# A bank ring ordered by end of filling, another order of the first loads, and query splitting moved from GpSimd to VectorE

## What is computed

```python
x = x + attention(layernorm(x), Wqkv, Wo)   # 32 query heads of 16, ONE shared key/value head
x = x + ffn(layernorm(x), W_base, b_base, W_gate, A, B)   # base matmul + top-2 of 8 LoRA experts, rank 16
# attention, for each batch b and head h:
#   scores = q @ k.T / 4 + slope[h] * (pos_k - pos_q), causal mask, softmax, @ v; all heads @ Wo
```

## Time and profile before

| what | us |
|---|---|
| median of three runs | 748.17 |
| the profiled execution | 748.7 |
| its span, first to last instruction | 746.9 |
| busy: PE / DVE / ACT / POOL | 686.0 / 557.4 / 359.2 / 228.9 |
| mean granted TensorE clock | 0.975 of full |

### The profile page before, as it was taken

The page is one execution under the profiler, slowest core; times in us unless marked ns, Lnnn a source line. Parts: engine busy times, 40 slices in busy tenths (PEclk is TensorE's granted clock), DMA queues, the critical chain, the costliest instruction groups (busy, mean ns, idle before and its releaser), DMA issues.

```text
span 746.9 us, 13261 instructions
## 1 busy us (share of the span) xinstructions
PE 686.0 (92%) x4304; PEld 309.7 (41%) x4304; DVE 557.4 (75%) x1801; ACT 359.2 (48%) x511; POOL 228.9 (31%) x382
## 2 busy tenths in 40 slices
PE   4689789999998989898989999999999999999997
PEld 2334434444443434343434334344334345555553
DVE  5679788867785868686879999999995175666665
ACT  2202556565554656464656666676676711111111
POOL 0027513132424351424243142143152132222221
PEclk9869999999999999998989999999999999999999
DMA  8641444443312160711070755910000049900001
GB/s 256 156 81 58 94 60 65 83 63 77 129 38 82 38 118 21 128 68 39 16 123 31 110 76 82 127 48 18 17 33 17 16 117 174 189 29 28 29 29 56
DMA packets 38343, 56.32 MB, mean 75 GB/s; under 512 B 6648, under 2 KB 20088, under 8 KB 38144
## 3 DMA queue, kind: packets, MB, share of 16 engines
q1 hardware_dynamic: 33896, 44.98, 32.0%
q0 software_dynamic: 1792, 6.29, 2.5%
q10 hardware_dynamic: 2592, 4.26, 1.6%
HBM read 35.72 MB, written 19.79 MB: 74 GB/s over the span
## 4 chain that ended last, share of the span: by engine, by line
PE 76%; DVE 11%; ACT 5%; DMA 3%; issue 3%; POOL 1%; SPq 1%; POOLq 0%; DVEq 0%; ACTq 0%
PE psum L728 18%; PE psum L680 16%; PE psum L710 11%; PE psum L756 7%; PE psum L627 7%; PE psum L778 6%; PE psum L707 4%; DVE psum L1091 3%; ACT work L913 3%; DVE negm L1096 3%; PE psum L773 2%; PE psum L788 2%; DMA x_sb<-in_x 1%; DMA q_dram<-arena 1%; PE psum L765 1%
## 5 line engine op out<-in xcount | busy, mean ns | idle before, releaser
L913 ACT ACTIVATE work<-psum 128x1024 f32<-128x1024 f32 (+1 forms) x320 | 289.0, 943 | 157.0 <-PE psum L710 122.2
L1091 DVE CUSTOM_DVE_ANT_0 psum<-psum,future 128x384 f32<-128x384 f32 (+3 forms) x512 | 238.8, 514 | 48.0 <-PE psum L680 44.5
L680 PE MATMUL psum<-k_op,arena 106*128 106x512 bf16 (+3 forms) x768 | 216.0, 335 | 26.0 <-DVE negm L1091 8.1
L1096 DVE TENSOR_REDUCE negm<-psum 128x1 f32<-128x512 f32 x256 | 167.2, 687 | 26.8 <-PE psum L680 23.9
L728 PE MATMUL psum<-work,v_op 128*32 128x512 f32 (+3 forms) x1536 | 168.1, 511 | 13.7 <-POOL work L1280 13.7
L1280 POOL TENSOR_SCALAR_AFFINE_SELECT work<-work 128x512 f32<-128x512 f32 x128 | 80.9, 637 | 285.7 <-ACT work L913 285.7
L710 PE MATMUL psum<-arena,k_op 109*128 109x512 bf16 (+3 forms) x640 | 157.6, 317 | 1.9 <-ACT work L913 1.4
L680 PEld LDWEIGHTS psum<-k_op,arena 106*128 106x128 bf16 x768 | 70.6, 98 | 171.3 <-DVE negm L1091 65.0
L627 PE MATMUL psum<-arena,wqkv_sb 128*128 128x256 f32 (+3 forms) x240 | 87.7, 473 | 1.3 <-ACT arena L835 1.3
L707 PE MATMUL psum<-arena,k_op 116*128 116x128 bf16 x512 | 84.9, 223 | 2.7 <-ACT arena L835 1.5
L710 PEld LDWEIGHTS psum<-arena,k_op 109*128 109x128 bf16 x640 | 59.7, 98 | 43.2 <-ACT work L913 13.8
(11 more groups left out here) (87 smaller groups left out, 466.1 us busy)
## 6 DMA issues: line engine op xcount, KB each, us to landing
arena<-q_dram SPq DMA_DIRECT2D x96, 128.0 KB, 5.6
o_dram<-o_sb SPq DMA_DIRECT2D x32, 256.0 KB
q_dram<-arena POOLq DMA_DIRECT2D x16, 384.0 KB, 3.2
arena<-o_dram SPq DMA_DIRECT2D x32, 128.0 KB, 8.8
arena<-rcp_dram SPq DMA_DIRECT2D x32, 128.0 KB, 9.4
out<-wqkv_sb ACTq DMA_DIRECT2D x16, 256.0 KB, 2.0
x_sb<-in_x SPq DMA_DIRECT2D x3, 1024.0 KB, 8.1
work<-in_x SPq DMA_DIRECT2D x3, 1024.0 KB, 16.9
```

The costliest lines, as they stand in the source:

```text
L680: last = nc.tensor.matmul(bank[:, a * width:(a + 1) * width], q_op[0:ROW_MAX, bass.ds(col, P)], k_op[0:ROW_MAX, b, k0:k0 + width], start=T ...
L913: nc.scalar.activation(probs[:, n % 4, heads * hp:heads * (hp + 1), 0:w], src, ACT.Exp).then_inc(exp_done, 1)
L1091: last = nc.vector.tensor_tensor_reduce(keys, keys, future[:, CH - width:CH], -1.0, 3e38, ALU.add, ALU.min, negm[:, late, 0, j * QT + t:j ...
L1096: nc.vector.tensor_reduce(dst, psum[:, bank, 0:len(js) * width].rearrange("p (a k) -> p a k", a=len(js)), AX_X, ALU.max, negate=True).then ...
```

## The change

Five things are changed.

1. `places` hands out banks by a list: a bank goes back to its end when a slot is placed, and for a side item when its last part is placed. With it the planner's extra limit on slots inside a side item goes, so a slot may now stand ahead of every part.
2. Items move: in step 0 chunk 0's queries come first, and two of chunk 1 stand behind the T items of chunk 2; slots of step 0 are spread to its end. The second item of step 4 goes to step 5 and so on, so steps 5 to 9 hold one query item each (before: step 4 two, steps 5 to 8 one).
3. DVE splits items 8 to 15, in steps 3 to 10 behind slot 8; POOL keeps items 2 to 7.
4. All stores of queries are issued by SP instead of POOL, each behind the wait for the store ahead of it.
5. SP's first loads: chunk 3's x comes behind the loads of items 0 and 1; the loads of items 2 to 5 now stand, each behind its store, ahead of `max_rows(1)`. Later loads of items 10 to 15 and of the heads come up to two steps later. DVE splits item 0 two tiles of normalising earlier.

```diff
 AMONG = {
-    0: [("v", 1, None, None)] + [("q", c, m, None) for m in (1, 2, 3) for c in (0, 1)] + tiles_turned(2),
+    0: [("v", 1, None, None)] + [("q", 0, m, None) for m in (1, 2, 3)] + [("q", 1, 1, None)] + tiles_turned(2) + [
+        ("q", 1, 2, None), ("q", 1, 3, None)],
...
-    4: [("v", 3, None, None)] + halves("q", 2, 1) + halves("q", 3, 1),
-    5: halves("q", 2, 2),
+    4: [("v", 3, None, None)] + halves("q", 2, 1),
+    5: halves("q", 3, 1),
...
-        upto = min(NSL - 1, round(NSL * done / (SLOTS_BY * total)))
-        if piece[0] == "side" and piece[2]:
-
-            if k:
-                upto = max(put, min(upto, put + NSB - 1 - inside))
-            inside += len(slots[put:upto])
-        else:
-            inside = 0
+        upto = min(NSL - 1, round(NSL * done / ((SLOTS_BY if k else 1) * total)))
...
+    banks = list(range(NSB))
     for k, order in enumerate(ORDER):
         for what, a, b in order:
...
+            if what == "slot":
+                bank = banks.pop(0)
+                slot_at[a, b] = (bank, last[bank])
+                last[bank] = ("slot", NSL * a + b)
+                banks.append(bank)
+            elif what == "side" and a >= N_FIRST:
+                if b == 0:
+                    bank = banks.pop(0)
                     use_at[a] = (bank, last[bank])
                     last[bank] = ("side", a)
+                if b == len(use_parts(USES[a])) - 1:
+                    banks.append(use_at[a][0])
...
-SPLIT_AT = {(3, 0): 8, (4, 0): 9, (4, 1): 10, (5, 0): 11, (5, 1): 12, (6, 1): 13, (7, 1): 14, (8, 1): 15}
+SPLIT_SLOT = 8
+ON_VECTOR = (0, 1) + tuple(range(8, NCH * PAIRS))
+SPLIT_AT = {3: 8, 4: 9, 5: 10, 6: 11, 7: 12, 8: 13, 9: 14, 10: 15}
...
+            def store_queries(n):
+
+                c, m = Q_ITEMS[n]
+                sp.wait_ge(*split_done(n))
+                if n:
+
+                    sp.wait_ge(q_stored, 16 * n)
+                sp.dma_start(q_dram[c, :, P * m:P * (m + 1)].rearrange("a r q -> r a q"),
+                             qpart[:, n % 4]).then_inc(q_stored, 16)
...
             load_x(2)
+            for n in range(2):
+                store_queries(n)
+                load_queries(n)
             load_x(3)
-            load_queries(0)
-            load_queries(1)
             load_constants(1)
-            step(0)
+            store_queries(2)
+            max_rows(0)
             load_queries(2)
-            load_queries(3)
-            step(1)
-            load_queries(4)
-            load_queries(5)
+            for n in range(3, 6):
+                store_queries(n)
+                load_queries(n)
+            store_queries(6)
+            store_queries(7)
+            max_rows(1)
             load_constants(2)
             load_constants(3)
-            step(2)
             load_queries(6)
             load_queries(7)
+            step(1)
+            step(2)
...
                     step(k, None, (r,))
                     if k % 2 == 0 and r % 4 == 3 and r // 4 < KEY_PIECES:
                         split_keys(k // 2 + 1, r // 4)
+                    if r == SPLIT_SLOT and k in SPLIT_AT:
+                        split_queries(SPLIT_AT[k])
```

More of the change, by code:

```diff
@@ L135 @@
     3: halves("kv", 3) + halves("q", 3, 0),
-    4: [("v", 3, None, None)] + halves("q", 2, 1) + halves("q", 3, 1),
-    5: halves("q", 2, 2),
-    6: halves("q", 3, 2),
-    7: halves("q", 2, 3),
-    8: halves("q", 3, 3),
+    4: [("v", 3, None, None)] + halves("q", 2, 1),
+    5: halves("q", 3, 1),
+    6: halves("q", 2, 2),
+    7: halves("q", 3, 2),
+    8: halves("q", 2, 3),
+    9: halves("q", 3, 3),
 }
@@ L209, in places @@
     slot_at, use_at, last = {}, {}, [None] * NSB
-    e = 0
     for u in range(N_FIRST):
         use_at[u] = (NSB + u % (8 - NSB), ("side", u - (8 - NSB)) if u >= 8 - NSB else None)
+    banks = list(range(NSB))
     for k, order in enumerate(ORDER):
         for what, a, b in order:
[L215 to L221, removed]
+            if what == "slot":
[6 more added lines that the diff above has]
+                    bank = banks.pop(0)
                     use_at[a] = (bank, last[bank])
                     last[bank] = ("side", a)
+                if b == len(use_parts(USES[a])) - 1:
+                    banks.append(use_at[a][0])
     return slot_at, use_at
 SLOT_AT, USE_AT = places()
-SPLIT_AT = {(3, 0): 8, (4, 0): 9, (4, 1): 10, (5, 0): 11, (5, 1): 12, (6, 1): 13, (7, 1): 14, (8, 1): 15}
+SPLIT_SLOT = 8
+ON_VECTOR = (0, 1) + tuple(range(8, NCH * PAIRS))
+SPLIT_AT = {3: 8, 4: 9, 5: 10, 6: 11, 7: 12, 8: 13, 9: 14, 10: 15}
 def uses_behind(k):
@@ L406, in use_count, with split_done @@
             return USES.index((kind, c, m, part)) + 1
+        def split_done(n):
+            if n in ON_VECTOR:
+                return q_split_v, ON_VECTOR.index(n) + 1
+            return q_split_p, n - 1
         TURNED = {c: use_count("T", c, QT - 1) for c in range(NCH)}
@@ L525, in step @@
                 if k < NK:
+                    if k in SPLIT_AT:
+                        store_queries(SPLIT_AT[k])
                     max_rows(2 * k, i)
@@ L566, in _ @@
             step(7)
+            load_queries(10)
+            load_queries(11)
             step(8)
+            step(9)
             load_queries(12)
             load_queries(13)
-            step(NB + 1)
+            load_sums(0)
+            step(10)
+            store_rcps(0)
+            step(11)
             load_queries(14)
             load_queries(15)
-            load_sums(0)
-            step(NB + 2)
-            store_rcps(0)
             load_heads(0)
-            step(NB + 3)
+            step(12)
             load_heads(1)
-            for k in range(NB + 4, NK + 2):
+            for k in range(13, NK + 2):
                 step(k)
@@ L673, in max_slot @@
                 if s == 0 and r in (0, EARLY_SLOTS):
-                    pe.wait_ge(q_in[1 if r else 0], 96 * (PAIRS * b + g + 1))
+                    n = Q_ITEMS.index((2 * b + late, g))
+                    pe.wait_ge(q_in[n % 2], 96 * (n // 2 + 1))
                 width = P * (t + 1) if kind == "diag" else CH
@@ L841, in query_hi @@
                 if not half:
[L842 to L846, removed]
+                    if n >= 2:
+                        act.wait_ge(*split_done(n - 2))
                 nc.scalar.mul(q4[:, n % 2, columns], psum[:, USE_AT[u][0], 0:CH if half is None else CH // 2], QSCALE
@@ L1101, in reciprocals @@
                 nc.vector.reciprocal(sums[:], sums[:]).then_inc(rcp_ready, 1)
-            for c in range(2):
-                statistics(c)
-                normalised(c, range(QT))
+            statistics(0)
+            normalised(0, range(QT))
+            statistics(1)
+            normalised(1, (0, 1))
             split_queries(0)
+            normalised(1, (2, 3))
             dve.wait_ge(w_in, 16 * N_W)
@@ L1114, in _ @@
                 step(0, None, (r,))
-                if 2 <= r < 2 + KEY_PIECES:
-                    split_keys(1, r - 2)
-                if r == EARLY_SLOTS + 2:
+                if 3 <= r < 3 + KEY_PIECES:
+                    split_keys(1, r - 3)
+                if r == 10:
                     normalised(2, (0, 1))
-                if r == EARLY_SLOTS + 6:
+                if r == 12:
                     normalised(2, (2, 3))
@@ L1133, in _ @@
                         split_keys(k // 2 + 1, r // 4)
+                    if r == SPLIT_SLOT and k in SPLIT_AT:
+                        split_queries(SPLIT_AT[k])
             for k in range(5, NK):
-                step(k)
+                for r in range(NSL):
+                    step(k, None, (r,))
+                    if r == SPLIT_SLOT and k in SPLIT_AT:
+                        split_queries(SPLIT_AT[k])
                 if k == NB + 2:
```

19 lines of the change are left out of this document (1 added, 18 removed).

## The result

The changed kernel is slower: 756.87 us (median of 6 runs, 752.95 to 759.30) against 747.28 (6 runs), a ratio of 1.0122 with a 95% interval of 1.0092 to 1.0153. 735.3 was forecast. The profiled execution took 756.69 us, its span is 754.9, 8.0 more than before.

What follows compares the result with a forecast made beforehand. PE was taken to bound E-to-L stretches, PE and DVE both L-to-E. Terms 7.3 - 3.7 - 18.2 + 1.7 = -12.9 us gave 735.3 us, with an 8 in 10 range of 719 to 744.

Steps and rivals of the forecast that it cites:

- The sum: Whole kernel: all terms added, -12.9 us, so 735.3 us against the median of 748.17.
- term put at nothing: Later loads and heads' loads on SP: said to land in time or stand beside no others, cost nothing.
- the term of steps 5 to 9: Steps 5 to 9: stalls for POOL and their clock losses go, 32.0 us per step, -18.2 us in all.
- The chain on SP: Start to step 1's end: serial loads and stores delay step 0's late maxima, PE waits 13 us; +7.3 us net.
- the chain is short: Rival, chance 0.15: stores pass loads or PE is later, so step 1's late scores begin at 82.9; 719.6 us.
- so long that all is lost: Rival, chance 0.05: four serial load-and-store turns before step 0's late maxima take 14 us each; 755 us.
- Steps 2 to 4: Steps 2 to 4: fewer waits on banks and an item less in step 4, together -3.7 us.
- DVE's splits cost twice: Rival, chance 0.10: DVE's split operations wait for POOL's triangles, 1.8 us more in each of eight L-to-E stretches; up to 749.7.
- Step 10: Step 10: the last split on DVE, in the stretch where DVE is a bound, adds 1.7 us.
- The ring: New bank list: ends PE's waits of 0.47 us per half item for ACT; the rival that it does nothing had 0.05.
- The rival on the slower side: Same rival as "so long that all is lost": first SP chain with turns of 14 us, 755 us, chance 0.05.

Runs made afterwards that it cites:

- e1_heads: Changed kernel with chunk 0's heads' loads behind step 10 and loads of query items 14 and 15 behind step 11 in SP's order; 747.08 us.
- e2_first: Changed kernel with SP's query stores 3 to 7 in a row, then step 0's late maxima, and the loads of items 3 to 7 after those; 740.97 us.
- e6_pool_stores: e1_heads with POOL instead of SP issuing the stores of items 2 to 7, each behind its split; 738.95 us.
- e3_both: Changed kernel with the edits of e1_heads and e2_first together; 731.34 us.
- e5_old_ring: e4_pool_split with banks handed out in strict turn and the planner's limit, as in the kernel before; 720.25 us.
- e4_pool_split: e3_both with query items 8 to 15 split by POOL again, behind the early maxima of steps 3 to 10; 710.46 us.
- e8_before_moved: Kernel before with POOL's splits of items 8 to 15 behind early maxima, one item per step in 5 to 9, some loads later; 726.20 us.

## Why the prediction was wrong, point by point

**The sum missed by 20.9 us, -12.9 against +8.0 in the spans.** Two steps of it failed: a term put at nothing (13.0 us) and the term of steps 5 to 9 (7.7 us). With the first alone put right (e1_heads) the kernel is as fast as before (ratio 0.9997) and not faster, so the second step matters as well.

**The term put at nothing** is this sentence: "The loads that come later by two steps land at least a step ahead of their use, and the heads' loads go beside steps that have no other: nothing." It looked only at when the loaded data are needed, and not at what they stand ahead of in SP's queue. Items 14 and 15 and the heads of chunk 0 were put in one place, 28 loads, ahead of step 12's maxima. This cost 13.0 us in the stretch; e1_heads removed it. That the heads' loads "go beside steps that have no other" was wrong by the change itself, which puts those of items 14 and 15 right in front of them. And the trace of the kernel before had the warning. There the rows of maxima of step 12 stood behind sixteen loads of heads alone and took 11.0 us:

```profile
474.87 0.38 SPq L485 DMA_DIRECT2D m_dram<-m_part  x1
485.87 0.25 SPq L492 DMA_DIRECT2D arena<-m_dram  x1
```

The turn after them came at 488.47, so 2.6 us were left, less than the 6 us that one more item's loads fill the queue by the prediction's own count; two items were added. The same argument had been made, with the right numbers, for the start of SP's queue. The Trainium skill, DMA: Bandwidth & Descriptors, Queues, rings and completion order, says that each DMA engine takes the descriptors of a ring in order; with that the trace agrees, 12 KB having landed after 15.6 us in the changed kernel and after 1.5 where the queue was empty (458.43 to 459.94).

**The chain on SP was right**, in mechanism and size: maxima back at 95.51 (95.9 forecast), the wait 12.8 us (13), step 1's late turn at 123.99 (124.5). That the loads and stores ahead of them in SP's queue hold the maxima back is shown by e2_first; e6_pool_stores shows the shares of load and store in a turn. The rivals "the chain is short" and "so long that all is lost" are out. PE's first slot came at 33.5 instead of 32.1 and the early turn at 51.54 instead of 50.1: item 0 was stored at 23.13, where I had 21.6 or so, since DVE waited 2.60 us for ACT's cast of that item and did not save the 1 us of its own order. The chain hid this.

**Steps 2 to 4 were right** to 0.4 us in the sum.

**Steps 5 to 9 were mis-sized.** The term was -18.2 and measured -10.5. The five stalls for POOL did go. Three things make up the 7.7 us.

First, the price of the split, 1.8 us in the sum for L-to-E. The stretches at full clock took 12.36 to 12.48 us instead of 11.9, and the split in them 2.3 to 2.4 us (next paragraph). Behind it DVE has no pause until the turn (from 303.76 to 311.00 in the stretch from 298.64), so the sum of its work set the end of the stretch, as forecast, but with a larger term. That is about 2.7 us in the five.

Second, the clock, about 2.8 us. DVE has to empty the three banks of the slots, and 2.4 us of other work in a row leaves PE without a bank: PE stood for 1.5 to 1.6 us ahead of the first part of the query item, in each of the five steps. In two of them it was then granted the half rate for a part of the stretch (mean clock 0.90 and 0.88, length 13.62 and 14.05), in the others not. I had counted the loss of the clock for POOL's stalls and forgot it for DVE's.

Third, E-to-L, 102.7 us in the five against 5 x 20.1, so 2.2. Half an item was put at "about as much" as the 1.6 us of L-to-E. PE is busy there for 20.27 us against 17.91 without an item, 2.4 more, and in the trace of the kernel before (242.34 to 262.96) it already was for 19.99.

**"DVE's splits cost twice"** held in part. Around 235 to 385 us the three operations took 0.87, 0.76 and 0.75 us, 2.4 together, where 1.8 was the price without POOL beside them:

```profile
L1063 DVE TENSOR_TENSOR arena<-arena 128x512 f32<-128x512 f32 x5 | 4.4, 873 | 0.0
L1064 DVE CAST arena<-arena 128x512 bf16<-128x512 f32 x5 | 3.8, 763 | 0.2
L1065 DVE TENSOR_TENSOR arena<-arena 128x512 bf16<-128x512 f32 x5 | 3.8, 754 | 0.2
```

That is 0.6 us more per item, and not 1.8. They took longer where POOL worked beside them: in the stretch from 298.64 triangles ran on POOL from 304.62 to 305.26 and from 306.04 to 306.75; the first and the third operation, which overlap them, took 0.87 and 1.00 us, the copy between them 0.43.

**Step 10 was right** in this execution (29.6, forecast 29.3), in part by luck: in the profiles of e1_heads, e2_first and e3_both it took 31.1 to 31.2 us, its L-to-E stretch at a clock of 0.88 or 0.89. **The ring** was right in sign. It is worth 9.8 us, in e5_old_ring against e4_pool_split, of which the forecast knew the waits on ACT; the rest is open.

The rival on the slower side named one mechanism (the first chain) with a chance of 0.05. Much of the slowdown came by the same mechanism at another place. That its 755 us lie near the measured 756.87 is chance: it needed turns of 14 us, and they took 8.5.

## What to carry to other kernels

When a DMA is moved, ask two questions: when its data are needed, and which small urgent transfer now stands behind it in the same queue. Count the bytes ahead of each one. When work is moved to an engine that has spare time on average, look at its longest unbroken block against the buffers between that engine and the one that is full; in pieces the splits cost a third of what they cost in a block (6.9 against 20.9 us), partly because the operations got cheaper too. And where a wait comes from an in-order engine, try another place on the same engine first: here that gave 21.4 us (e8_before_moved, with the items spread), while the same splits on VectorE instead of POOL cost 20.9 (e3_both against e4_pool_split).

## What the runs showed that I had not expected

Whether the half rate follows a short stall is not settled by its length alone. Stalls of 1.5 to 1.6 us ahead of the query item were followed by it in some stretches and not in others of the same execution, which made stretches of the same instructions 12.4 or 14.0 us long, and probably made runs of such kernels spread (752.95 to 759.30 in six runs of the change) where those without the stall spread less (709.01 to 710.95 in four of e4_pool_split). The kernel before, with POOL's stalls, spread too: its two runs near 739 us had a mean clock of 0.99, the other 17 one of 0.972 to 0.981. I can't say from these runs what decides between the two.
